# Sparse attention on one Trainium2 core: strided keys and values of all groups kept on chip, a unit's own keys and values loaded with its queries

## What is computed

```python
def _sparse_attn(q, k, v, M):            # BLOCK = 128, GBL = 8, 16 heads, d = 16
    k_str = k[:, :, :Lg].reshape(B, Hn, ns, GBL, d)[:, :, :, -1, :]     # every 8th key
    v_str = v[:, :, :Lg].reshape(B, Hn, ns, GBL, d)[:, :, :, -1, :]
    ...
    fk = jnp.concatenate([jnp.broadcast_to(k_str[:, :, None], (B, Hn, nb, ns, d)), fk_loc], axis=-2)
    fv = jnp.concatenate([jnp.broadcast_to(v_str[:, :, None], (B, Hn, nb, ns, d)), fv_loc], axis=-2)
    w = jnp.einsum('bhnqd,bhnkd->bhnqk', fq, fk) * scale + fmask
    w = jax.nn.softmax(w, axis=-1)
    o1 = jnp.einsum('bhnqk,bhnkd->bhnqd', w, fv).reshape(B, Hn, L, d)
```

## Time and profile before

| what | value |
|---|---|
| median of 3 runs | 5355.12 us (5348.21 to 5361.87) |
| the profiled execution | 5351.09 us |
| its span, first to last instruction | 5349.2 us |
| mean granted TensorE clock | 0.916 |
| stage 1 | 0 to 212 us |
| sparse stage | 212 to 971 us |
| middle stage | from 973 us |
| TensorE busy | 4794.5 us |

### The profile page before, as it was taken

The page is one execution under the profiler, slowest core; times in us unless marked ns, Lnnn a source line. Parts: engine busy times, 40 slices in busy tenths (PEclk is TensorE's granted clock), DMA queues, the critical chain, the costliest instruction groups (busy, mean ns, idle before and its releaser), DMA issues.

```text
span 5349.2 us, 82616 instructions
## 1 busy us (share of the span) xinstructions
PE 4794.5 (90%) x31872; PEld 2551.8 (48%) x31872; DVE 4064.9 (76%) x9211; ACT 2852.4 (53%) x3317; POOL 284.4 (5%) x339
## 2 busy tenths in 40 slices
PE   5377989676599999999999999999999999899999
PEld 4244445566244333443334443333443333588888
DVE  7465757577488898889998888998889977455555
ACT  3234545322155666666676666677566777432322
POOL 2010000133000000000000000000000000300000
PEclk8778989887578999999999999999999999899999
DMA  4633221355600030030120210200300000201010
GB/s 151 172 72 66 43 53 27 111 189 192 125 17 13 7 52 12 21 54 9 15 38 15 40 32 9 37 16 23 59 10 5 9 9 10 69 21 40 21 40 9
DMA packets 226730, 255.84 MB, mean 48 GB/s; under 512 B 69329, under 2 KB 170705, under 8 KB 224017
## 3 DMA queue, kind: packets, MB, share of 16 engines
q1 hardware_dynamic: 216512, 190.12, 12.5%
q0 software_dynamic: 9824, 60.43, 7.0%
HBM read 143.99 MB, written 104.92 MB: 47 GB/s over the span
## 4 chain that ended last, share of the span: by engine, by line
PE 70%; DVE 19%; issue 5%; DMA 4%; ACT 2%; SPq 1%; POOL 0%; DVEq 0%; ACTq 0%; POOLq 0%
PE psum L782 22%; PE psum L713 19%; PE psum L76 13%; DVE maxes_dense L862 11%; PE psum L741 4%; PE psum L679 3%; PE psum L702 2%; DMA queries_sparse<-neg_rows_sparse 1%; PE psum L723 1%; PE psum L750 1%; PE psum L1541 1%; DVE masked_scores_dense L855 1%; DMA x_in<-in_L_attn_hidden_states 1%; DMA keys_sparse<-parts_scratch 1%; PE psum L709 1%
## 5 line engine op out<-in xcount | busy, mean ns | idle before, releaser
L819 ACT ACTIVATE probs_dense<-psum 128x1024 f32<-128x1024 f32 (+3 forms) x2304 | 2068.4, 950 | 996.7 <-PE psum L741 746.7
L862 DVE TENSOR_REDUCE maxes_dense<-psum 128x1 f32<-128x512 f32 x3584 | 2227.8, 683 | 227.3 <-PE psum L713 226.2
L713 PE MATMUL psum<-keys_dense,queries_dense 48*128 48x512 f32 (+3 forms) x4608 | 1553.6, 477 | 138.1 <-DMA queries_dense<-parts_scratch 54.8
L713 PEld LDWEIGHTS psum<-keys_dense,queries_dense 48*128 48x128 f32 x4608 | 667.5, 191 | 1490.8 <-DVE maxes_dense L862 1142.1
L782 PE MATMUL psum<-probs_dense,values_dense 128*32 128x512 f32 (+3 forms) x9216 | 1176.6, 588 | 0.0
L741 PE MATMUL psum<-queries_dense,keys_dense 50*128 50x512 f32 (+3 forms) x4608 | 809.3, 407 | 11.8 <-ACT probs_dense L819 11.5
L855 DVE CUSTOM_DVE_ANT_0 masked_scores_dense<-psum,causal_add 128x128 f32<-128x128 f32 (+3 forms) x1024 | 452.2, 488 | 175.6 <-PE psum L713 156.0
L741 PEld LDWEIGHTS psum<-queries_dense,keys_dense 50*128 50x128 f32 x4608 | 448.6, 193 | 106.8 <-ACT probs_dense L819 60.8
L855 DVE CUSTOM_DVE_ANT_0 masked_scores_sparse<-psum,after_add 128x512 f32<-128x512 f32 x512 | 326.4, 688 | 173.2 <-PE psum L702 172.2
L1648 ACT ACTIVATE activated<-psum 128x512 f32<-128x512 f32 x208 | 124.7, 599 | 414.1 <-PE psum L76 401.6
L819 ACT ACTIVATE probs_sparse<-psum 128x1024 f32<-128x1024 f32 x224 | 217.6, 1022 | 207.3 <-PE psum L679 78.9
(11 more groups left out here) (297 smaller groups left out, 5379.9 us busy)
## 6 DMA issues: line engine op xcount, KB each, us to landing
v_scratch<-ve_s SPq DMA_DIRECT2D x96, 256.0 KB, 2.7
parts_scratch<-part_high SPq DMA_DIRECT2D x24, 1024.0 KB, 4.2
parts_scratch<-part_low SPq DMA_DIRECT2D x24, 1024.0 KB, 6.7
queries_dense<-parts_scratch SPq DMA_DIRECT2D x384, 64.0 KB
keys_dense<-parts_scratch POOLq DMA_DIRECT2D x42, 512.0 KB, 17.7
values_dense<-v_scratch POOLq DMA_DIRECT2D x8, 2048.0 KB, 34.5
queries_sparse<-parts_scratch SPq DMA_DIRECT2D x192, 64.0 KB
keys_sparse<-parts_scratch POOLq DMA_DIRECT2D x18, 512.0 KB, 17.6
```

Source lines behind the costliest of these rows:

```text
L713: m = pe.matmul(bank[:, 0:width], q[rows(h, TROWS), h // 2, b * P:(b + 1) * P], k[rows(h, TROWS), h // 2, kc * STRIP:kc * STRIP + width], ...
L819: act.activation(probs[i % 6][:, :, first_col:STRIP], psum[:, at2:at2 + 2, first_col:STRIP], ACT.Exp, scale=SCALE, **extra).then_inc(exp_d ...
L862: m = dve.tensor_reduce(mx[:, h * BLOCKS + b, kc:kc + 1], bank, AX.X, ALU.max)
```

## The change

Stage 1 gets a step more. GpSimd copies every eighth column of the key half of `part_high` and `part_low` into a small tile (`take_strided`), and SP stores it with two DMAs per strip into `strided_scratch` (256 rows by 512 tokens, high and low). ScalarE and VectorE wait for that copy before they write the parts of the next strip. The masks of the sparse stage are loaded in stage 1, ahead of the second input strip.

In the sparse stage the strided keys and values of all four groups get a buffer each and are loaded by SP at the stage's start, seven DMAs a group, from `strided_scratch` and `v_scratch`. The whole groups' `keys` and `values` are gone, and with them GpSimd's loads and `compact` on ScalarE. In their place stand four buffers of a unit's own keys (512 tokens) and values. `load_queries` brings them too: 13 DMAs a unit instead of 6, all on `queries_in`. The matmuls are the same, in the same order, and read other tiles.

```diff
+            def take_strided(s):
+                pool.wait_ge(part_low_set, 2 * (s + 1))
+                pool.wait_ge(part_high_set, 4 * (s + 1))
+                if s >= 1:
+                    pool.wait_ge(strided_stored, 32 * s)
+                for i, part in enumerate((part_high, part_low)):
+                    pool.tensor_copy(strided[:, i, :, :], part[:, DC:2 * DC, STRIDE - 1::STRIDE].bitcast(F32)).then_inc(strided_set, 1)
...
+                sp.wait_ge(strided_set, 2 * (s + 1))
+                for i in range(2):
+                    dst = str_d[i][:, s * (STRIP // STRIDE):(s + 1) * (STRIP // STRIDE)].rearrange("(m p) t -> p m t", p=P)
+                    sp.dma_start(dst, strided[:, i, :, :]).then_inc(strided_stored, 16)
...
+                    if sparse:
+                        for odd in range(2):
+                            for i, (_, part) in enumerate(TERMS):
+                                src = parts_d[a][part][DIM + g * GROUP * HEAD_DIM:DIM + (g + 1) * GROUP * HEAD_DIM, j * STRIP:(j + 1) * STRIP]
+                                first_row = odd * HALF + i * HEAD_DIM
+                                sp.dma_start(keys[n % held][first_row:first_row + HEAD_DIM, :, :].bitcast(F32),
+                                             src.rearrange("(h o e) t -> o e h t", o=2, e=HEAD_DIM)[odd]).then_inc(queries_in[n % 8], 16)
+                        sp.dma_start(values[n % held][:], v_d[a][g, j * STRIP:(j + 1) * STRIP, :].rearrange("(b p) n -> p b n", p=P)).then_inc(queries_in[n % 8], 16)
...
                 if sparse:
-                    load_keys(sp, 0, slice(0, TOKENS), first_keys_in)
                     load_queries(0)
+                    load_strided(0)
+                    for tile in with_ones:
+                        load_ones(tile, ones_in)
+                    for g in range(1, GROUPS):
+                        load_strided(g)
...
-                            pe.wait_ge(queries_in[n % 8], 128 * ((past + n) // 8) + 96)
-                            wait_keys(n)
+                            pe.wait_ge(queries_in[n % 8], earlier + per_unit * (n // 8) + loads)
                             if sparse:
-                                pe.wait_ge(compacted, 2 * (n // STRIPS + 1))
+                                pe.wait_ge(str_in[n // STRIPS], 16 * 7)
...
-                    for odd in range(2):
-                        own = slice(odd * HALF, odd * HALF + SROWS)
-                        act.activation(str_keys[group % 2][own, :, :], keys[group % 2][own, :, STRIDE - 1::STRIDE].bitcast(F32),
-                                       ACT.Copy).then_inc(compacted, 1)
...
-                load_values(pool, 0)
-                load(1)
+                    load_values(pool, 0)
+                    load(1)
```

More of the change, by code:

```diff
@@ L478, in attend @@
         held = 4 if sparse else 8
+        loads = 16 * (13 if sparse else 6)
+        per_unit = loads + 32
+        earlier = 0 if sparse else 4 * (16 * 13 + 32)
         groups = [(a, g) for a in jobs for g in range(GROUPS)]
@@ L547, in attend @@
         with ExitStack() as st:
-            keys_in, values_in, str_in = ([sem(f"{k}_{stage}_in{i}") for i in range(2)] for k in ("keys", "values", "strided"))
-            first_keys_in = sem(f"first_keys_{stage}_in")
-            masks_in, bias_set = sem(f"masks_{stage}_in"), sem(f"after_bias_{stage}_set")
+            if sparse:
+                str_in = [sem(f"strided_in{g}") for g in range(GROUPS)]
+                ones_in, bias_set = sem("ones_sparse_in"), sem("after_bias_set")
+            else:
+                keys_in, values_in = ([sem(f"{k}_in{i}") for i in range(2)] for k in ("keys", "values"))
+                first_keys_in, masks_in = sem("first_keys_in"), sem("masks_in")
             side_filled, side_freed = sem(f"side_filled_{stage}"), sem(f"side_freed_{stage}")
@@ L553, in attend @@
             split_done = sem(f"split_{stage}")
-            compacted = sem("strided_keys_set") if sparse else None
-            keys = [sbuf(st, f"keys_{stage}_{i}", [P, PAIRS, TOKENS], F32R) for i in range(2)]
-            values = [sbuf(st, f"values_{stage}_{i}", [P, TOKENS // P, GROUP * GCOL]) for i in range(2)]
+            if sparse:
+                keys = [sbuf(st, f"own_keys_{i}", [P, PAIRS, STRIP], F32R) for i in range(held)]
+                values = [sbuf(st, f"own_values_{i}", [P, BLOCKS, GROUP * GCOL]) for i in range(held)]
+            else:
+                keys = [sbuf(st, f"keys_{i}", [P, PAIRS, TOKENS], F32R) for i in range(2)]
+                values = [sbuf(st, f"values_{i}", [P, TOKENS // P, GROUP * GCOL]) for i in range(2)]
             queries = [sbuf(st, f"queries_{stage}_{i}", [P, PAIRS, STRIP], F32R) for i in range(held)]
@@ L566, in attend @@
             aos = [sbuf(st, f"aos_{stage}_{i}", [P, BLOCKS, GROUP * HEAD_DIM]) for i in range(2)]
-            masks = []
             masked_scores = [sbuf(st, f"masked_scores_{stage}_{i}", [P, STRIP]) for i in range(2)]
-            if not sparse:
+            if sparse:
+                str_keys = [sbuf(st, f"str_keys_{g}", [P, PAIRS, NSTR], F32R) for g in range(GROUPS)]
+                str_values = [sbuf(st, f"str_values_{g}", [P, NSTR // P, GROUP * GCOL]) for g in range(GROUPS)]
+                after_bias = sbuf(st, "after_bias", [P, 1])
+                eye2 = eye2_h
+                with_ones = str_keys + keys
+            else:
                 causal_add = sbuf(st, "causal_add", [P, STRIP], BF16)
@@ L659, in wait_keys @@
                     pe.wait_ge(first_keys_in, 96)
-                    if not sparse and n >= 1:
+                    if n >= 1:
                         pe.wait_ge(keys_in[0], 96)
                 else:
-                    pe.wait_ge(keys_in[group % 2], 96 * (group // 2 + (1 if group % 2 or not sparse else 0)))
+                    pe.wait_ge(keys_in[group % 2], 96 * (group // 2 + 1))
             def attend_pe():
@@ L686, in attend_pe @@
                     a, g, j = units[n]
-                    k, q = keys[n // STRIPS % 2], queries[n % held]
-                    v = values[n // STRIPS % 2]
+                    slot = n % held if sparse else n // STRIPS % 2
+                    k, v, q = keys[slot], values[slot], queries[n % held]
                     if kind in ("tile", "hand", "out"):
@@ L749, in attend_pe @@
                                 own, full = rows(odd, SROWS), pair[odd]
[L750 removed]
+                                m = pe.matmul(full, str_keys[n // STRIPS][own, h // 2, c * P:(c + 1) * P], q[own, h // 2, :],
                                               start=True, stop=not partly)
@@ L916, in attend_pool @@
                     pool.tensor_tensor(low, part, high.bitcast(F32), ALU.subtract).then_inc(split_done, 1)
-                for group in range(2, len(groups)):
-                    load(group)
+                if not sparse:
+                    for group in range(2, len(groups)):
+                        load(group)
             attend_sp()
```

115 lines of the change are left out of this document (64 added, 51 removed).

## The result

The changed kernel takes 5225.4 us (median of 4 runs, 5214.5 to 5241.9) against 5352.4 us (4 runs) for the kernel before: a ratio of 0.9744, 95% interval 0.9716 to 0.9772. The forecast was 5220 with a range of 5195 to 5285. The profiled execution took 5214.5 us, its span is 5212.6, so 136.6 us went between the two profiles.

A forecast was written before the change was run, and what follows sets the result against it. TensorE, busy 90% of the span, was taken as the bound, so gains must remove its work or waits. 5351.1 - 91.4 - 18.5 - 32 + 8 + 2 = 5219, stated as 5220, range 5195 to 5285.

The forecast's parts named there:

- Parts 1 and 2: Sparse stage rhythm: no bulk loads between units saves 91.4 us, no strided copies on ScalarE saves 18.5 us.
- part 4: Sparse units: seven more DMAs ahead of each hand DMA (negated row maxima into the queries) cost 8 us, bounds 0 to 56.
- part 1: Sparse stage: without bulk loads between units, three long hand distances become common ones, saving 91.4 us.
- part 2's sign: Sparse stage, ScalarE's strided copies gone: no distance of hands near 23 us but at the start.
- margin of 1.2 us: Sparse units: time between the end of the 13 DMAs' landing, about 860, and the next hand's issue at 861.27.
- a rival of its own: Sparse units: hand DMA somewhat late, 42 to 56 us instead of 8, total 5254 to 5270, up to 5285; chance 0.14.
- Part 3: Start of the sparse stage: smaller loads let work begin earlier, first hand landed at 256 instead of 287.74, saving 32 us.
- Rival C: Sparse stage's start gives little: unit 0's hand lands at 270 or later, total 5234, or 5250 with clock lost; chance 0.06.
- Part 5: Stage 1: the added copies and strided stores cost 1 us at the stage's end and 2 elsewhere, bounds 0 and 10.
- Both signs of part 5: Stage 1: strips as far apart as before, and last base store landed within 2 us of where it was.
- the 0.9 asked for: Sparse stage: the prediction falls if the stage's clock stays under 0.9.

The follow-up runs named there:

- r1_changed_again: The changed kernel itself, unedited, run again as the measure of later runs: 5238.5 us, ratio 0.9772 to the kernel before.
- e4: The changed kernel with each unit's six own key DMAs loaded a second time, 19 DMAs a unit instead of 13: 5267.9 us, ratio 0.9822.
- e5: The changed kernel with each unit's six own key DMAs loaded twice more, 25 DMAs a unit: 5377.9 us, ratio 1.0052.
- y_both: The changed kernel with a new DMA order at the sparse stage's start and stage 1's input strips loaded a strip earlier: 5214.1 us, ratio 0.973.
- e1_bulk: The changed kernel with GpSimd's three bulk loads of keys and values put back, into tiles nothing reads: 5312.1 us, ratio 0.9916.
- e7_masks: The changed kernel with the nine mask loads moved behind stage 1's third base store: 5241.4 us, ratio 0.9787.

## Why the prediction was right

**Parts 1 and 2** were summed at 109.9 us, less 8 for late hands (part 4). The rhythm lost 107.1 us. The three bulk loads put back cost 86.5 us of distance against the 91.4 of part 1, the copies 21.4 against 18.5, of which 9 are shown as waits. The mechanism is right. That the number fits this well is in part luck: the forecast took the undisturbed distance of 17.84 us for all, and the clock kept to that in the first profile, while in r1_changed_again the rhythm is 18.2 us longer without any wait. There part 2's sign, no distance near 23 us, fails too: it has distances of 24.99, 23.63, 23.55 and 23.63 us with no copy in them.

**Part 4** held. SP's burst takes 6.2 us (285.94 to 292.16; forecast 6.15), SP then pauses 2.8 us until the hand, and no hand is late. The 8 us charged weren't spent. The transfers were the longer of the two, as the prediction's own 6.6 us against 6.15 of issue says (it calls them "under the issue time"). In a later unit the burst is issued from 595.21 and the next hand at 603.97, and the DMA engines come to rest only then:

```profile
602.00:603.00 1.00, 1.00 (x9) 0.50 (x11) 0.83 (x3) 0.10 (x1) 0.00 (x0) 1.00 0.79 194
603.00:604.00 1.00, 1.00 (x18) 0.85 (x16) 0.94 (x5) 0.41 (x1) 0.00 (x0) 1.00 0.31 91
604.00:605.00 1.00, 1.00 (x15) 0.52 (x16) 0.29 (x1) 1.00 (x2) 0.00 (x0) 1.00 0.00 0
```

So the margin of 1.2 us was under 1. That it was worth a rival of its own is shown by e4 and e5: six DMAs more eat the margin, twelve more eat the gain. The Trainium skill, "DMA: Bandwidth & Descriptors" (Anatomy of one DMA), gives a fixed time for each DMA that GpSimd issues. It doesn't say that the times of several add up, and for the 13 that SP issues here they don't: they and their landing fit in 9 us, as the trace of before had it.

**Part 3** had the right mechanism and sizes off: 32 us forecast, 26.1 measured. Two terms were small. The ones DMAs were put at 0.45 us of issue; they take 0.63 (5.17 and 4.96 for eight each), 3 us more in all. And stage 1 ended later than the 1 us allowed: the first issue is at 215.79, not 213. With 1 us more for the other 54 issues (0.47 us each) they move the second unit's last issue from 244.5 to 251.5. TensorE's wait was foreseen at 5 us and is 12.46, because the data came 7.8 us later than put (254.26 against 246.5); the tiles before it ended when they should (241.8 against 242). One term was too large and gave 2.3 us back: the hand was put at 5 us from issue to use and took 2.7 (259.03 to 261.69). Rival C, at 5234, describes the direction, though its hand at 270 didn't come.

**Part 5** was too low: 1 and 2 us were set down, 4.9 came (base store at 209.96 against 205.05 in rows 4). The step that failed is the pricing of the strided stores by the landing of the value stores alone. Their issue was taken to fit into the 1.7 us between the part stores and the base store; it takes SP 2.0 us in the last strip and 2.4 in the one before. Both signs of part 5 fail, the strips' distance and the 2 us on the last base store. The line of the Trainium skill, "DMA: Bandwidth & Descriptors" (Specifications), on transfers under 512 bytes pointed the right way, but no run here separates a slow write from a slow issue.

The errors nearly cancel. In the profiled execution: 5219 as forecast, 6 more for the start, 5 less for the rhythm (107.1 saved, 101.9 forecast net of late hands), 2 less that were set down for stage 1 beside the start and lie in it already, and 3.6 less behind the last hand, make 5214.4; measured are 5214.5. That the median lies 5 us from the forecast is this cancelling and the clock together: the second series of the same kernel has a median of 5238.5, 18 us off and still in the range. The clock in the rhythm was 0.97, over the 0.9 asked for, and 0.93 in r1_changed_again.

## What to carry to other kernels

A small DMA on which the busiest engine waits should not have a bulk load beside it: here, cutting a group's load into units, each issued behind the small DMA of the unit before, removed three waits of 20 to 25 us. Before adding loads to such a queue, compare their issue time with the free stretch until the next small DMA; past that point the price was steep here, since the waits also cost clock. When two versions differ by waits and by clock, compare TensorE's idle time first: it repeated within 1 us over seven profiles, while the rhythm's length varied by 34. At a stage's start, put into the queue first what the second piece of work needs, and only then what is needed much later.

## What the runs showed of the hardware that was not expected

Here many short waits of TensorE cost more clock than a few long ones. From the first to the last hand, for the same matmuls (us):

| profile | rhythm | TensorE idle | TensorE busy | clock |
|---|---|---|---|---|
| before | 662.9 | 95.7 | 567.2 | 0.87 |
| changed, first | 555.8 | 17.0 | 538.8 | 0.97 |
| r1_changed_again | 574.0 | 16.9 | 557.1 | 0.93 |
| y_both | 589.2 | 16.5 | 572.7 | 0.90 |
| e1_bulk | 655.6 | 92.5 | 563.1 | 0.87 |
| e5_more12 | 696.2 | 53.0 | 643.2 | 0.79 |

In e1 three waits of 73 us in all leave the busy time where kernels without them have it; in e5 36 us more of idleness, spread over the units, go with 70 to 104 us more of it.

The clock also falls without any wait. This is a stretch of y_both, hand to hand, in which TensorE has no wait of 0.3 us or more:

```profile
363.10:386.66 23.56, 23.24 (x163) 11.61 (x161) 14.31 (x42) 10.39 (x12) 0.00 (x0) 0.71 0.21 53
```

TensorE is busy 23.24 of 23.56 us and yet its clock averages 0.71, where the same 163 matmuls take 17.17 us in an undisturbed distance. Such distances come one behind the other, three of 23.6 in r1_changed_again, none in the first profile of the same kernel. They make most of the 18 us between these two profiles. That they make much of the spread of the runs too, 5214 to 5242 us, isn't shown, since each kernel has one trace. Their places aren't all chance: in r1_changed_again, e7_masks and y_both they are the 22nd to 24th distance. What sets them off isn't known from these runs.
